# Starting TensorE on ones and loading x first in a two-layer attention kernel

## The chip, the cores and the metric

The kernel runs on 1 core of a Trainium2 chip. The metric is the device time of one execution in microseconds; three executions were timed, and one more was taken with the hardware profiler.

## The reference

Two attention layers follow one another on x (2 images of 32 x 32 positions and 256 channels, float32). One layer is:

```python
xn = group_norm(x, gamma, beta)                  # 32 groups of 8 channels
q, k, v = (xn @ w + b for w, b in ((wq, bq), (wk, bk), (wv, bv)))
attn = softmax(q @ k.T / sqrt(256))              # over the 1024 positions of an image
out = (attn @ v) @ wp + bp + x
```

## The kernel before

**Algebra.** Per layer A is made from wq and wk (with bk as one column more), Wx from wv and wp. The scores are xn times t, where t = A times xn plus a vector. V is xn times Wx. Each float32 operand of these products is split into a high and a low fp32r part: ScalarE writes the high part from PSUM, VectorE subtracts it for the low one. A product is then three fp32r matmuls. The products of weights themselves and the transposes are plain float32.

**Work.** A unit is one image in one layer (UNITS = 4), and has two chunks of 512 queries. Per unit: transpose the rows of x (four pieces r of 256 rows), statistics, group mean and variance by small matmuls into bank Z, gain and shift (affine_map), normalise in four quarters q = (h, k), xn_high and xn_low, four t products (h, k), eight values, and per chunk eight scores, the maxima, the exponentials and attention.

**Order.** Each engine has its own in-order list, written out by hand, and waits on semaphores. There are no loops that a planner orders. What matters here is the start, up to scores(0, 0) and the first transposes of image 1:

- SP (L238 to L245) loads wq and wk of layer 0, image 0 in four pieces, wv and wp, layer 1's wq and wk, wide(0) (bq, bk and bp of layer 0 on all partitions), layer 1's wv and wp, wide(1), image 1. Each is one DMA of 256 KB, wide 384 KB.
- TensorE (L806 to L837, then L969) transposes wq, the small vectors, wk, then the four pieces of x through ring[2] and ring[3] in turn, with A_product(0, 0) behind the third and A_product(0, 1) behind the fourth; then wv, wq(1) and wk(1), mean_of_groups, Wx_product(0, 0), variance_of_groups, Wx_product(0, 1), wv(1), output_bias of both layers, the A and the Wx products of layer 1, the four t products of unit 0, and scores(0, kb), with next_rows(1, kb) (transposes of image 1 into Z) behind each of the first four.
- ScalarE (L344 to L362, then L390) follows with weight_transposed (PSUM to SBUF), raw_rows, A_high, Wx_high, xn_high and t_high.
- VectorE (L557 to L585, then L637) follows with statistics_of, A_low, attention_vector, group_deviation, variance, affine_map, normalise(0) for all four quarters, Wx_low, the four xn_low, output_bias of both layers, attention_vector(1), A_low(1), Wx_low(1), and the four t_low of unit 0.
- GpSimd makes the constants, the power (L273) and, from the first output bias on, the eight residuals (L279) of unit 0.

t_product (L856) waits for the low parts of its half and takes four PSUM banks ring[0] to ring[3]. scores(0, kb) (L884) waits for t_low of its half. next_rows (L898) waits at r == 0 for both output biases on VectorE (L902), since these read Z.

Of the kernel before, what the change touches and what calls it, by code (L numbers as in the profile page):

```python
# [11 lines left out]
P = 128  # L12
# [7 lines left out]
def two_attention_layers(nc, x, layers, vectors, out):  # L20
# [13 lines left out]
    LAYERS = len(layers)  # L34
    UNITS = IMAGES * LAYERS
    KC = C // P
    NB = N // P
    HALVES = N // BANK
# [39 lines left out]
    with ExitStack() as ctx:  # L78
# [6 lines left out]
        def sem(name):  # L85
            return ctx.enter_context(nc.semaphore(name))
# [102 lines left out]
        ac_P = sem("ac_P")  # L189

        dv_const = sem("dv_const")
        dv_vec = sem("dv_vec")
# [28 lines left out]
        @block.sync  # L221
        def _(sp):
            def load_image(b):
                for r in range(NR):
                    sp.dma_start(xnat[:, b, 2 * r:2 * r + 2, :], x_rows[b, :, 2 * r:2 * r + 2, :]
                                 ).then_inc(ld_x[b][r], 16)

            def load_weights(l, names):
                for name in names:
                    sp.dma_start(w_raw[l, name][:], layers[l][name].rearrange("(k p) d -> p k d", p=P)  # L230
                                 ).then_inc(ld_w[l, name], 16)

            def load_wide(l):
                at = VECTORS.index(WIDE[0])
                sp.dma_start(wide[:, l], vectors_of_layer[:, l, at:at + len(WIDE), :].to_broadcast([P, len(WIDE), C])
                             ).then_inc(ld_wide[l], 16)

            load_weights(0, ("wq", "wk"))  # L238
            load_image(0)
            load_weights(0, ("wv", "wp"))  # L240
            load_weights(1, ("wq", "wk"))
            load_wide(0)
            load_weights(1, ("wv", "wp"))
            load_wide(1)
            load_image(1)  # L245

            for u in range(UNITS - IMAGES, UNITS):
                for i in range(NB):
                    sp.wait_ge(dv_O, u * NB + i + 1)
                    sp.dma_start(out_rows[u % IMAGES, :, i, :], xnat[:, u % IMAGES, i, :]).then_inc(stored, 16)  # L250
            sp.wait_ge(stored, 16 * IMAGES * NB)
# [57 lines left out]
        def _(act):  # L309
# [33 lines left out]

            weight_transposed(0, 0)  # L344
            weight_transposed(0, 1)
            for r in range(NR):
                raw_rows(0, r, ring[2 + r % 2])
                if r == 2:
                    A_high(0, 0)
            A_high(0, 1)  # L350
            weight_transposed(0, 2)
            weight_transposed(1, 0)
            weight_transposed(1, 1)
            for k in range(KC):
                Wx_high(0, k)
            weight_transposed(1, 2)
            for q in range(TQ):
                xn_high(0, q)
            A_high(1, 0)
            A_high(1, 1)  # L360
            for k in range(KC):
                Wx_high(1, k)  # L362

# [25 lines left out]

            for h in range(HALVES):  # L390
                for k in range(KC):
                    t_high(0, h, k)
            for kb in range(NB):
# [63 lines left out]
        @block.vector  # L457
        def _(dve):
            nc.vector.memset(minus_half[:], -0.5)
            for v in V:  # L460
# [80 lines left out]

            def normalise(v):
                dve.wait_ge(dv_stat, v * STAT + SHIFT)
                for q in range(TQ):
                    h, k = divmod(q, KC)
# [4 lines left out]
            def xn_low(v, q):  # L550
# [8 lines left out]
                                  ).then_inc(dv_vec, 1)  # L559
            statistics_of(0, 0)  # L560
            statistics_of(0, 1)
            statistics_of(0, 2)
            A_low(0, 0)
            statistics_of(0, 3)
            channel_statistics(0)
            A_low(0, 1)
            attention_vector(0, 0)
            group_deviation(0)
            attention_vector(0, 1)
            variance(0)  # L570
            Wx_low(0, 0)
            attention_vector(0, 2)
            affine_map(0)
            normalise(0)
            Wx_low(0, 1)
            for q in range(TQ):
                xn_low(0, q)
            for l in range(LAYERS):
                output_bias(l)
            for n in range(NATT):  # L580
                attention_vector(1, n)
            for k in range(KC):
                A_low(1, k)
            for k in range(KC):
                Wx_low(1, k)  # L585

# [49 lines left out]

            for h in range(HALVES):  # L637
                for k in range(KC):
                    t_low(0, h, k)
            for kb in range(1, NB):  # L640
# [107 lines left out]
        def _(pe):  # L748
# [22 lines left out]
            def Wx_product(l, mc):  # L771
                pe.wait_ge(ac_wT, 3 * l + 3)
                pe.wait_ge(ld_w[l, "wp"], 16)
                if l == 0:
                    pe.wait_ge(ac_xT, NR - KC + mc + 1)
                bank = ring[2 + mc][:, 0:C] if l == 0 else X[:, mc * C:(mc + 1) * C]
# [25 lines left out]
            def variance_of_groups(v):  # L802
                pe.wait_ge(dv_stat, v * STAT + VARC)
                nc.tensor.matmul(Z[:, 0:KC], group_mean[:], var_c[:], start=True, stop=True).then_inc(pe_gv, 1)

            pe.wait_ge(po_const, 5)  # L806
            transpose_weight(0, 0)
            pe.wait_ge(ld_vec, 16)
            for k in range(KC):
                last = nc.tensor.transpose(X[:, k * LAYERS * NV:(k + 1) * LAYERS * NV],  # L810
                                           vec_rows[:, k * P:(k + 1) * P], ident[0:LAYERS * NV, 0:LAYERS * NV])
            last.then_inc(pe_vec, 1)
            transpose_weight(0, 1)
            for r in range(NR):
                pe.wait_ge(ld_x[0][r], 16)
                if r >= 2:
                    pe.wait_ge(ac_xT, r - 1)
                transpose_rows(ring[2 + r % 2], 0, r)
                if r == 2:
                    A_product(0, 0)  # L820
            A_product(0, 1)
            transpose_weight(0, 2)
            transpose_weight(1, 0)
            transpose_weight(1, 1)
            mean_of_groups(0)
            Wx_product(0, 0)
            variance_of_groups(0)
            Wx_product(0, 1)
            transpose_weight(1, 2)
            pe.wait_ge(dv_stat, VARE)  # L830
            for l in range(LAYERS):
                output_bias(l)
            for mc in range(KC):
                A_product(1, mc)
            pe.wait_ge(ac_wT, 6)
            for mc in range(KC):
                Wx_product(1, mc)  # L837

# [17 lines left out]
            def t_product(u, h, k):  # L856
                l = u // IMAGES
                if k == 0:
                    pe.wait_ge(dv_xl, u * TQ + (h + 1) * KC)
                wait_for_bank("t", u, h, k)  # L860
                bank = bank_of("t", u, h, k)
# [106 lines left out]

            for h in range(HALVES):  # L969
                for k in range(KC):  # L970
                    t_product(0, h, k)
            for kb in range(NB):
# [96 lines left out]
```

## Time and profile before

| | us |
|---|---|
| median of 3 executions | 280.77 |
| lowest, highest | 280.07, 282.04 |
| profiled execution | 281.29 |
| its span, first to last instruction | 279.4 |
| mean granted TensorE clock | 0.988 |

The profiled execution's own time is 1.89 us longer than its span. Its durations and start times are those of that one execution. Start times below are microseconds from the span's start. PE is TensorE's matmul side, PEld its weight loads, DVE is VectorE, ACT is ScalarE, POOL is GpSimd, SP the engine that issues the loads. PEclk is the granted clock as a share of 2.4 GHz.

### The profile page before, as it was taken

The numbers are of one execution on the slowest core, as the hardware profiler recorded it, in microseconds if no ns is written. First come the engines' busy times: TensorE is split into PE (matmuls) and PEld (weight loads), VectorE is DVE, ScalarE is ACT, GpSimd is POOL, SyncE is SP. The second block draws the span as 40 slices with busy tenths as digits, with TensorE's granted clock in tenths as the row PEclk, the third lists the DMA queues.
The fourth block names the chain that finished last, engine by engine and source line by source line (L and its number), as shares of the span: only waits on it lengthen the run. The fifth ranks groups of instructions, "written<-read, shape, count | busy, mean of one in ns | idle before, by whom it ended". The sixth has DMA issues, their size and how long they took to land.

```text
span 279.4 us, 4591 instructions
## 1 busy us (share of the span) xinstructions
PE 261.8 (94%) x1650; PEld 235.6 (84%) x1650; DVE 176.3 (63%) x440; ACT 148.4 (53%) x291; POOL 110.6 (40%) x111
## 2 busy tenths in 40 slices
PE   3999999969987999999999999999999999999994
PEld 2887889849977899977998899977998899889993
DVE  0699568895568455755879455755978446564623
ACT  3564444757158734573377724573377615670660
POOL 2017101355135551552055651552055652560680
PEclk9999999996999999999999999999999999999999
DMA  5950000000000000000000000000000000100102
GB/s 163 366 188 1 0 1 2 0 0 2 0 0 4 1 0 2 0 0 2 1 0 1 2 2 0 0 2 0 33 27 19 1 21 19 38 2 19 40 19 75
DMA packets 5965, 7.37 MB, mean 26 GB/s; under 512 B 556, under 2 KB 4664, under 8 KB 5944
## 3 DMA queue, kind: packets, MB, share of 16 engines
q1 hardware_dynamic: 5920, 7.08, 7.5%
q8 instruction: 13, 0.21, 0.3%
q14 instruction: 8, 0.07, 0.1%
q10 hardware_dynamic: 24, 0.01, 0.0%
HBM read 4.99 MB, written 2.10 MB: 25 GB/s over the span
## 4 chain that ended last, share of the span: by engine, by line
PE 66%; DVE 21%; issue 6%; ACT 5%; DMA 1%; POOL 0%; DVEq 0%; ACTq 0%; POOLq 0%
PE ring L892 8%; PE ring L894 8%; PE ring L893 8%; PE O L931 7%; PE O L933 7%; PE O L932 7%; DVE xraw L547 4%; DVE S L625 3%; DVE xnat L635 3%; DVE xn_lo L554 2%; PE ring L878 2%; PE ring L931 2%; PE ring L933 2%; PE ring L932 2%; DVE t_lo L590 2%
## 5 line engine op out<-in xcount | busy, mean ns | idle before, releaser
L284 POOL TENSOR_TENSOR P_lo<-S,P_hi 128x512 fp32r<-128x512 f32 x64 | 83.0, 1303 | 118.3 <-ACT S L388 118.3
L931 PE MATMUL O<-V,P_hi 128*128 128x258 f32 x208 | 60.5, 291 | 0.0
L933 PE MATMUL O<-V,P_lo 128*128 128x258 f32 x208 | 59.4, 285 | 0.0
L932 PE MATMUL O<-V,P_hi 128*128 128x256 f32 x208 | 59.3, 285 | 0.0
L380 ACT COPY S<-ring 128x512 f32<-128x512 f32 x64 | 37.5, 586 | 39.7 <-PE ring L894 37.9
L387 ACT ACTIVATE P_hi<-S 128x512 fp32r<-128x512 f32 x64 | 40.5, 633 | 26.3 <-DVE S L625 26.3
L892 PE MATMUL ring<-t_hi,xn_lo 128*128 128x512 f32 x128 | 51.5, 403 | 0.8 <-DVE t_lo L590 0.8
L894 PE MATMUL ring<-t_hi,xn_hi 128*128 128x512 f32 x128 | 50.1, 392 | 0.0
L893 PE MATMUL ring<-t_lo,xn_hi 128*128 128x512 f32 x128 | 50.0, 391 | 0.0
L608 DVE TENSOR_TENSOR R<-ring,R 128x512 f32<-128x512 f32 x48 | 33.0, 687 | 25.4 <-ACT S L380 25.1
L625 DVE TENSOR_TENSOR S<-X,S 128x512 f32<-128x512 f32 x64 | 42.1, 681 | 0.0
L932 PEld LDWEIGHTS O<-V,P_hi 128*128 128x128 f32 x208 | 40.0, 192 | 0.5
L931 PEld LDWEIGHTS O<-V,P_hi 128*128 128x128 f32 x208 | 40.0, 192 | 0.5
L933 PEld LDWEIGHTS O<-V,P_lo 128*128 128x128 f32 x208 | 40.1, 193 | 0.0
L388 ACT ACTIVATE S<-S 128x512 f32<-128x512 f32 x64 | 39.8, 623 | 0.0
L892 PEld LDWEIGHTS ring<-t_hi,xn_lo 128*128 128x128 f32 x128 | 24.1, 188 | 5.5 <-DVE t_lo L590 1.2
L894 PEld LDWEIGHTS ring<-t_hi,xn_hi 128*128 128x128 f32 x128 | 24.0, 188 | 5.3
L893 PEld LDWEIGHTS ring<-t_lo,xn_hi 128*128 128x128 f32 x128 | 24.1, 189 | 4.3
L366 ACT ACTIVATE t_hi<-ring,att 128x512 fp32r<-128x512 f32 x16 | 10.7, 683 | 29.4 <-PE ring L867 29.4
L279 POOL TENSOR_TENSOR xnat<-xnat,out_bias 128x256 f32<-128x256 f32 x32 | 23.0, 751 | 6.3 <-DVE out_bias L500 6.3
L878 PE MATMUL ring<-Wx_hi,xn_lo 128*128 128x258 f32 x64 | 18.8, 294 | 2.8 <-DVE w_row L599 2.0
L590 DVE SCALAR_TENSOR_TENSOR t_lo<-ring,att,t_hi 128x512 fp32r<-128x512 f32 x16 | 11.7, 746 | 13.1 <-ACT t_hi L366 13.1
(113 smaller groups left out, 417.5 us busy)
## 6 DMA issues: line engine op xcount, KB each, us to landing
xnat<-in_x SPq DMA_DIRECT2D x8, 256.0 KB, 6.7
out<-xnat SPq DMA_DIRECT2D x16, 128.0 KB, 1.9
wide<-in_vectors SPq DMA_DIRECT2D x2, 384.0 KB, 6.9
w_wq<-in_L_conv_wq SPq DMA_DIRECT2D x2, 256.0 KB, 4.8
w_wk<-in_L_conv_wk SPq DMA_DIRECT2D x2, 256.0 KB, 4.8
w_wv<-in_L_conv_wv SPq DMA_DIRECT2D x2, 256.0 KB, 6.6
w_wp<-in_L_conv_wp SPq DMA_DIRECT2D x1, 256.0 KB, 6.7
w_wp<-in_L_conv_wo SPq DMA_DIRECT2D x1, 256.0 KB, 6.7
```

The lines of the kernel that those rows point to most:

```text
L284: nc.gpsimd.tensor_tensor(P_lo[:, tile, :], S[:, tile, :], P_hi[:, tile, :].bitcast(F32), ALU.subtract).then_inc(po_P, 1)
L380: nc.scalar.copy(S[:, tile_of(c, kb), :], bank_of("S", c, kb)[:]).then_inc(ac_S, 1)
L387: nc.scalar.activation(P_hi[:, tile, :], S[:, tile, :], ACT.Exp)
L388: nc.scalar.activation(S[:, tile, :], S[:, tile, :], ACT.Exp).then_inc(ac_P, 1)
L608: nc.vector.tensor_tensor(R[:], bank_of("S", c, kb)[:], earlier, ALU.max).then_inc(dv_R, 1)
L625: nc.vector.tensor_tensor(tile, X[:], tile, ALU.add).then_inc(dv_D, 1)
L892: nc.tensor.matmul(bank[:], xn_lo[:, kc, keys], t_hi[:, kc, cols], start=(kc == 0), stop=False)
L893: nc.tensor.matmul(bank[:], xn_hi[:, kc, keys], t_lo[:, kc, cols], start=False, stop=False)
L894: last = nc.tensor.matmul(bank[:], xn_hi[:, kc, keys], t_hi[:, kc, cols], start=False, stop=(kc == KC - 1))
L931: nc.tensor.matmul(bank[:, 0:C + 2], P_hi[:, tile, mine], v[:, kb, 0:C + 2], start=(kb == 0), stop=False)
L932: nc.tensor.matmul(bank[:, 0:C], P_hi[:, tile, mine], v[:, kb, C + 2:VX], start=False, stop=False)
L933: last = nc.tensor.matmul(bank[:, 0:C + 2], P_lo[:, tile, mine], v[:, kb, 0:C + 2], start=False, stop=(kb == NB - 1))
```

## The change

SP's order becomes image 0, wq and wk, wide(0), wv and wp, all of layer 1, wide(1), image 1. VectorE first of all writes ones into R[:, 0:P]; TensorE multiplies them with themselves (8 matmuls before anything else, 2 behind each of the first three pieces of x), with the result in Z, which nothing reads before it is written again. The pieces of x come first on TensorE and go to the four banks ring[0] to ring[3], then the three weights of layer 0 are transposed. In the order of TensorE, both A products stand around variance_of_groups; transposing wv(1) and both output_bias stand behind the first two t products, and Wx_product(1) behind the last two. The t products of unit 0 wait in addition for A_low (first half) and for Wx_low (second half). ScalarE and VectorE follow that order; normalise takes a list of quarters and is done in two parts. On VectorE both A_low stand ahead of affine_map, and output_bias and attention_vector(1) behind Wx_low(1). On ScalarE weight_transposed(1, 2) stands ahead of xn_high(0, 2).

```diff
@@ -188,6 +188,7 @@
         ac_S = sem("ac_S")
         ac_P = sem("ac_P")
 
+        dv_ones = sem("dv_ones")
         dv_const = sem("dv_const")
         dv_vec = sem("dv_vec")
         dv_A = sem("dv_A")
@@ -235,12 +236,11 @@
                 sp.dma_start(wide[:, l], vectors_of_layer[:, l, at:at + len(WIDE), :].to_broadcast([P, len(WIDE), C])
                              ).then_inc(ld_wide[l], 16)
 
+            load_image(0)
             load_weights(0, ("wq", "wk"))
-            load_image(0)
+            load_wide(0)
             load_weights(0, ("wv", "wp"))
-            load_weights(1, ("wq", "wk"))
-            load_wide(0)
-            load_weights(1, ("wv", "wp"))
+            load_weights(1, ("wq", "wk", "wv", "wp"))
             load_wide(1)
             load_image(1)
 
@@ -341,25 +341,21 @@
                 cols = slice(h * BANK, (h + 1) * BANK)
                 nc.scalar.copy(xn_hi[:, k, cols], xraw[:, k, cols]).then_inc(ac_xh, 1)
 
-            weight_transposed(0, 0)
-            weight_transposed(0, 1)
             for r in range(NR):
-                raw_rows(0, r, ring[2 + r % 2])
-                if r == 2:
-                    A_high(0, 0)
-            A_high(0, 1)
-            weight_transposed(0, 2)
+                raw_rows(0, r, ring[r])
+            for n in range(3):
+                weight_transposed(0, n)
+            for k in range(KC):
+                A_high(0, k)
             weight_transposed(1, 0)
             weight_transposed(1, 1)
+            xn_high(0, 0)
+            xn_high(0, 1)
             for k in range(KC):
                 Wx_high(0, k)
             weight_transposed(1, 2)
-            for q in range(TQ):
-                xn_high(0, q)
-            A_high(1, 0)
-            A_high(1, 1)
-            for k in range(KC):
-                Wx_high(1, k)
+            xn_high(0, 2)
+            xn_high(0, 3)
 
             def t_high(u, h, k):
                 act.wait_ge(pe_t, u * TQ + h * KC + k + 1)
@@ -387,9 +383,14 @@
                 nc.scalar.activation(P_hi[:, tile, :], S[:, tile, :], ACT.Exp)
                 nc.scalar.activation(S[:, tile, :], S[:, tile, :], ACT.Exp).then_inc(ac_P, 1)
 
-            for h in range(HALVES):
-                for k in range(KC):
-                    t_high(0, h, k)
+            for k in range(KC):
+                t_high(0, 0, k)
+            for k in range(KC):
+                A_high(1, k)
+            for k in range(KC):
+                t_high(0, 1, k)
+            for k in range(KC):
+                Wx_high(1, k)
             for kb in range(NB):
                 score_copy(0, kb)
                 if kb < NR:
@@ -456,6 +457,7 @@
 
         @block.vector
         def _(dve):
+            nc.vector.memset(R[:, 0:P], 1.0).then_inc(dv_ones, 1)
             nc.vector.memset(minus_half[:], -0.5)
             for v in V:
                 nc.vector.memset(v[:, :, C:C + 2].bitcast(F32), 1.0)
@@ -539,9 +541,9 @@
                 dve.wait_ge(dv_stat, at + GMUL)
                 nc.vector.tensor_tensor(shift[:], beta, gain_mean[:], ALU.subtract).then_inc(dv_stat, 1)
 
-            def normalise(v):
+            def normalise(v, quarters=range(TQ)):
                 dve.wait_ge(dv_stat, v * STAT + SHIFT)
-                for q in range(TQ):
+                for q in quarters:
                     h, k = divmod(q, KC)
                     cols = slice(h * BANK, (h + 1) * BANK)
                     nc.vector.tensor_scalar(xraw[:, k, cols], xraw[:, k, cols], gain[:, k:k + 1], shift[:, k:k + 1],
@@ -557,32 +559,25 @@
             dve.wait_ge(pe_vec, 1)
             nc.vector.tensor_copy(vec_cols[:], X[:, 0:KC * LAYERS * NV].rearrange("p (k r) -> p k r", k=KC)
                                   ).then_inc(dv_vec, 1)
-            statistics_of(0, 0)
-            statistics_of(0, 1)
-            statistics_of(0, 2)
+            for r in range(NR):
+                statistics_of(0, r)
+            channel_statistics(0)
+            group_deviation(0)
+            attention_vector(0, 0)
+            variance(0)
             A_low(0, 0)
-            statistics_of(0, 3)
-            channel_statistics(0)
             A_low(0, 1)
-            attention_vector(0, 0)
-            group_deviation(0)
+            affine_map(0)
+            normalise(0, range(0, 2))
+            xn_low(0, 0)
+            xn_low(0, 1)
             attention_vector(0, 1)
-            variance(0)
-            Wx_low(0, 0)
+            normalise(0, range(2, 4))
+            for k in range(KC):
+                Wx_low(0, k)
+            xn_low(0, 2)
+            xn_low(0, 3)
             attention_vector(0, 2)
-            affine_map(0)
-            normalise(0)
-            Wx_low(0, 1)
-            for q in range(TQ):
-                xn_low(0, q)
-            for l in range(LAYERS):
-                output_bias(l)
-            for n in range(NATT):
-                attention_vector(1, n)
-            for k in range(KC):
-                A_low(1, k)
-            for k in range(KC):
-                Wx_low(1, k)
 
             def t_low(u, h, k):
                 dve.wait_ge(ac_t, u * TQ + h * KC + k + 1)
@@ -634,9 +629,18 @@
                 rows = xnat[:, (c // 2) % IMAGES, (c % 2) * QB + j, :]
                 nc.vector.scalar_tensor_tensor(rows, bank[:, 0:C], inv, rows, ALU.mult, ALU.add).then_inc(dv_O, 1)
 
-            for h in range(HALVES):
-                for k in range(KC):
-                    t_low(0, h, k)
+            for k in range(KC):
+                t_low(0, 0, k)
+            for k in range(KC):
+                A_low(1, k)
+            for k in range(KC):
+                t_low(0, 1, k)
+            for k in range(KC):
+                Wx_low(1, k)
+            for l in range(LAYERS):
+                output_bias(l)
+            for n in range(NATT):
+                attention_vector(1, n)
             for kb in range(1, NB):
                 running_max(0, kb)
                 if kb <= NR:
@@ -771,8 +775,6 @@
             def Wx_product(l, mc):
                 pe.wait_ge(ac_wT, 3 * l + 3)
                 pe.wait_ge(ld_w[l, "wp"], 16)
-                if l == 0:
-                    pe.wait_ge(ac_xT, NR - KC + mc + 1)
                 bank = ring[2 + mc][:, 0:C] if l == 0 else X[:, mc * C:(mc + 1) * C]
                 for kd in range(KC):
                     last = nc.tensor.matmul(bank, wvT[:, l, kd, mc * P:(mc + 1) * P],
@@ -803,38 +805,38 @@
                 pe.wait_ge(dv_stat, v * STAT + VARC)
                 nc.tensor.matmul(Z[:, 0:KC], group_mean[:], var_c[:], start=True, stop=True).then_inc(pe_gv, 1)
 
+            def keep_running(n):
+
+                for _ in range(n):
+                    nc.tensor.matmul(Z[:, 0:P], R[:, 0:P], R[:, 0:P], start=True, stop=True)
+
+            pe.wait_ge(dv_ones, 1)
+            keep_running(8)
             pe.wait_ge(po_const, 5)
-            transpose_weight(0, 0)
-            pe.wait_ge(ld_vec, 16)
-            for k in range(KC):
-                last = nc.tensor.transpose(X[:, k * LAYERS * NV:(k + 1) * LAYERS * NV],
-                                           vec_rows[:, k * P:(k + 1) * P], ident[0:LAYERS * NV, 0:LAYERS * NV])
-            last.then_inc(pe_vec, 1)
-            transpose_weight(0, 1)
             for r in range(NR):
                 pe.wait_ge(ld_x[0][r], 16)
-                if r >= 2:
-                    pe.wait_ge(ac_xT, r - 1)
-                transpose_rows(ring[2 + r % 2], 0, r)
-                if r == 2:
-                    A_product(0, 0)
+                transpose_rows(ring[r], 0, r)
+                if r == 0:
+                    pe.wait_ge(ld_vec, 16)
+                    for k in range(KC):
+                        last = nc.tensor.transpose(X[:, k * LAYERS * NV:(k + 1) * LAYERS * NV],
+                                                   vec_rows[:, k * P:(k + 1) * P], ident[0:LAYERS * NV, 0:LAYERS * NV])
+                    last.then_inc(pe_vec, 1)
+                if r < NR - 1:
+                    keep_running(2)
+            transpose_weight(0, 0)
+            transpose_weight(0, 1)
+            transpose_weight(0, 2)
+            mean_of_groups(0)
+            A_product(0, 0)
+            variance_of_groups(0)
             A_product(0, 1)
-            transpose_weight(0, 2)
             transpose_weight(1, 0)
             transpose_weight(1, 1)
-            mean_of_groups(0)
-            Wx_product(0, 0)
-            variance_of_groups(0)
-            Wx_product(0, 1)
-            transpose_weight(1, 2)
-            pe.wait_ge(dv_stat, VARE)
-            for l in range(LAYERS):
-                output_bias(l)
+            for mc in range(KC):
+                Wx_product(0, mc)
             for mc in range(KC):
                 A_product(1, mc)
-            pe.wait_ge(ac_wT, 6)
-            for mc in range(KC):
-                Wx_product(1, mc)
 
             def wait_for_bank(*tile):
 
@@ -857,6 +859,12 @@
                 l = u // IMAGES
                 if k == 0:
                     pe.wait_ge(dv_xl, u * TQ + (h + 1) * KC)
+                if u == 0:
+
+                    if h == 0:
+                        pe.wait_ge(dv_A, KC)
+                    else:
+                        pe.wait_ge(dv_Wx, KC)
                 wait_for_bank("t", u, h, k)
                 bank = bank_of("t", u, h, k)
                 cols = slice(h * BANK, (h + 1) * BANK)
@@ -966,9 +974,16 @@
                         wait_for_output_bank(c, j)
                     attend(c, j, kb)
 
-            for h in range(HALVES):
-                for k in range(KC):
-                    t_product(0, h, k)
+            for k in range(KC):
+                t_product(0, 0, k)
+            transpose_weight(1, 2)
+            pe.wait_ge(dv_stat, VARE)
+            for l in range(LAYERS):
+                output_bias(l)
+            for k in range(KC):
+                t_product(0, 1, k)
+            for mc in range(KC):
+                Wx_product(1, mc)
             for kb in range(NB):
                 scores(0, kb)
                 if kb < NR:
```

## Rows read from the trace of the kernel before

**Rows 1.** The page: busy share of the span by engine, and TensorE in 40 slices.

```profile
PE 261.8 (94%) x1650; PEld 235.6 (84%) x1650; DVE 176.3 (63%) x440; ACT 148.4 (53%) x291; POOL 110.6 (40%) x111
...
PE   3999999969987999999999999999999999999994
```

**Rows 2.** Busy time by stretch, TensorE: stretch, length, PE busy, PEclk, DMA share, GB/s.

```profile
7.30:10.20 2.90, 2.88 (x13) 1.00 1.02 352
59.30:61.80 2.50, 0.06 (x1) 0.94 0.00 0
61.80:68.40 6.60, 6.47 (x29) 0.50 0.01 2
```

**Rows 3.** Groups of weight loads (count, busy us, mean ns), then transposes in time order.

```profile
L758 PEld LDWEIGHTS O<-ident,w_wq 128*128 128x128 f32 x4 | 0.7, 216 | 3.7 <-issue 3.7
...
L793 PEld LDWEIGHTS ring<-ident,xnat 128*128 128x128 f32 x12 | 2.3, 221 | 1.8 <-DMA xnat<-in_x 1.5 <-issue 0.3
...
L793 PEld LDWEIGHTS ring<-ident,xnat 128*128 128x128 f32 x4 | 0.5, 140 | 0.1
...
11.07 0.60 PE L793 MATMUL ring<-ident,xnat 128*128 128x128 f32 x4
...
12.38 0.60 PE L758 MATMUL X<-ident,w_wv 128*128 128x128 f32 x4
...
12.82 0.60 PE L758 MATMUL O<-ident,w_wq 128*128 128x128 f32 x4
```

**Rows 4.** DMA: first piece of the chain, landing of x, volume from 0.

```profile
0.79 2.84 DMA w_wq<-in_L_conv_wq
...
DMA to landing us min/median/max: 5.5/6.7/7.6
...
0.00:6.60 6.60, 2.45 (x10) 1.71 (x10) 0.47 (x10) 2.22 (x3) 1.91 (x11) 1.00 0.57 155
0.00:10.10 10.10, 5.23 (x23) 4.21 (x24) 1.39 (x13) 3.63 (x5) 1.91 (x11) 1.00 0.71 220
```

**Rows 5.** Instructions in time order on TensorE: start, duration, form, idle time before.

```profile
18.12 1.90 PE L767 MATMUL O<-wkT_bk,wqT 128*128 128x257 f32 x8
19.86 1.89 PE L778 MATMUL X<-w_wp,wvT 128*128 128x256 f32 x8
21.39 0.58 PE L865 MATMUL ring<-xn_hi,A_lo 128*128 128x512 f32 x1
...
28.11 0.50 PE L892 MATMUL ring<-t_hi,xn_lo 128*128 128x512 f32 x1 [0.79 <-DVE t_lo L590]
```

**Rows 6.** The same on ScalarE and VectorE, from the third piece of x.

```profile
11.27 0.38 ACT L327 ACTIVATE A_hi<-ring 128x256 fp32r<-128x256 f32 x1 [0.36 <-PE ring L767]
11.75 0.42 DVE L478 SCALAR_TENSOR_TENSOR A_lo<-ring,A_hi 128x256 fp32r<-128x256 f32 x1
13.11 0.39 DVE L506 BATCH_NORM_AGGREGATE mv<-bn 128x2 f32<-128x24 f32 x2
14.54 0.16 DVE L518 TENSOR_TENSOR var_c<-dev,mv 128x2 f32<-128x2 f32 x1
...
16.24 0.16 DVE L529 TENSOR_TENSOR r0sq<-r 128x2 f32<-128x2 f32 x1
16.59 0.59 ACT L322 COPY wvT<-X 128x512 f32<-128x512 f32 x1
17.41 1.92 DVE L547 TENSOR_SCALAR xraw<-xraw,gain,shift 128x512 f32<-128x512 f32 x4
18.00 1.14 ACT L342 CAST xn_hi<-xraw 128x512 fp32r<-128x512 f32 x2 [0.82 <-DVE xraw L547]
```

**Rows 7.** The same, behind Wx(1).

```profile
21.78 0.65 ACT L334 CAST Wx_hi<-X 128x256 fp32r<-128x256 f32 x2 [0.94 <-PE X L778]
21.98 0.75 DVE L500 TENSOR_TENSOR out_bias<-Z,wide 128x256 f32<-128x256 f32 x2
...
26.00 0.74 DVE L487 TENSOR_TENSOR Wx_lo<-X,Wx_hi 128x256 fp32r<-128x256 f32 x2
```

## The prediction

> **What bounds the kernel now.** I read the page first: its busy line and its slices. TensorE (PE) is busy 94% of 279.4 us, and the slices show 9 tenths nearly everywhere; only the first and the last are low, and a few others a little [rows 1]. The change touches only what lies before the scores of the first unit, so the second view is the busy time by stretch. PE is idle until 3.8 and for 1.1 us before 7.3, works without a gap from there to 27.3, lacks 0.8 us before 28.11 [rows 5], and is then full until 59.3. A second hole of 2.4 us stands before 61.8, and behind it the granted clock is 0.50, the 1.2 GHz level, until 68.4 [rows 2]. So from 7.3 on the bound of the start is PE's own queue, and the end can come earlier only if scores(0, 0) starts before 28.11 us, or if less stands behind it.
>
> Third, the groups of weight loads by line, since they pace transposes. A load of a transpose takes 216 to 221 ns until 9.9 us and 140 ns from 10.8 us on; four of them stand 0.44 us after one another's start at the fast pace (12.38 and 12.82) [rows 3]. The granted clock is printed as 1.00 in both [rows 2], but the longer loads tell me the lower level, 1.2 GHz, before some 10.2 us. So four transposes take 0.9 us of PE at the lower level and 0.44 at the higher.
>
> **The change part by part.** The sum is made against the profiled execution: 281.29 us with a span of 279.4. The median of the runs shown is 280.77, so 0.52 is taken off at the end.
>
> *DMA order.* x now stands at the head of SP's queue, wq and wk behind it, then wide(0), wv and wp, then layer 1. An issue costs 0.43 to 0.5 us, as before, and the same bytes move. Lower bound for x0: the first transfer in the queue landed 2.84 us after its issue at 0.79, so 3.63 us [rows 4]. Upper bound: the transfers of x took 5.5 us at best, so 6.3 us. By volume: before, 6.6 us x 155 GB/s = 1.02 MB had moved by 6.6 us, which is all of x (1.05 MB) [rows 4]. I take the volume; x then keeps ahead of PE (below). wv of layer 0 ends at 2.23 MB, and 10.1 us x 220 GB/s is 2.22: it is there at 10.1 [rows 4].
>
> *Ones.* keep_running(8) is 8 fp32 matmuls of 128 columns. Two A products, four such calls, show as eight instructions [rows 5], so these are 16, each paced like a transpose: 16 x 0.227 = 3.6 us at the lower level, from about 1.05 (DVE writes the ones first of all) to 4.7. Three keep_running(2) add 4 instructions each, 0.44 us at the higher level, 0.91 at the lower. When does the clock rise? Two cases in the trace: PE dense from 7.3, fast by 10.2, 2.9 us; PE dense from 61.8, fast by 68.4, 6.6 us [rows 2]. From 1.05 that gives 4.0 to 7.7; I take the middle, 5.8. Until the last group of x, PE has 3 groups of x, 3 of ones (6 x 0.44) and the vectors (0.2): 2.9 us at the higher level. From 4.7, with 1.1 us at half speed, that puts the last transposes of x at 8.15 (7.3 for a rise at 4.0; 9.05 for 7.7; 10.5 if it doesn't rise in time). Before they were at 11.07 [rows 3]. So the head gains 2.9 us. x3 has landed by volume at 6.7: the ones cover the landing, and if it is late instead (6.3 for x0), the last group is at about 9.3.
>
> *From x to the first t product.* From those transposes to the aggregated statistics: 11.07 to 13.50 (13.11 + 0.39), 2.43 us, unchanged [rows 3, 6]. wq, wk and wv are transposed meanwhile (1.3 us) and are in. Statistics to var_c: 13.50 to 14.70 (14.54 + 0.16), 1.2 us [rows 6]. Then comes something new: VectorE takes both A_low ahead of affine_map. A_product(0, 1) stands behind variance_of_groups, so A(0, 1) ends 2.35 after the statistics (two products of 4 x 0.217 = 0.87, as eight take 19.86 - 18.12 = 1.74, with two small matmuls and the tail); A_high 0.38 + 0.17 and A_low 0.42 + 0.15 less overlap bring affine_map to 3.4, where before it was 16.24 - 13.50 = 2.7 [rows 5, 6]. The power on GpSimd ends earlier and isn't seen. Affine_map takes 1.17 us (16.24 to 17.41), xn_high starts 0.59 behind it (18.00), two of them take 1.14, the second xn_low 0.6: 2.35 [rows 6]. Now only two quarters are normalised ahead. In all 2.43 + 3.4 + 1.17 + 2.35 and hops = 9.5 us; before 21.39 - 11.07 = 10.3. t(0,0) starts at 17.65, 3.7 us earlier. From A(0, 1) to there PE has two weights to transpose, the pair of Wx and the pair of A(1), 0.88 + 1.73 + 1.74 = 4.35 us, in the 4.9 that it has: no bound.
>
> *Behind the first t products.* Before, four t products (24 matmuls, 27.3 less 21.39, 5.6) and the hole of 1.2 led to 28.11, 6.7 us [rows 5]. Now: two t products 2.78, the transposes of wv(1) 0.44, output_bias 1.73 (8 instructions), two t products 2.78, Wx(1) 1.73 = 9.5 us. The work is only moved: 3.9 us that stood ahead of the t products now stand between them and the scores. And it adds a wait. ScalarE has weight_transposed(1, 2) ahead of xn_high(0, 2) in its strict order, and that copy now waits for transposes that stand behind both first t products. So xn_high(0, 2) can't begin until 0.16 + 0.59 after them, then two xn_high 1.14 and an xn_low 0.6 with hops: 2.6 us, against 1.73 of output_bias as cover [rows 5, 6]. PE waits 0.85 us at t(1,0). Queued behind that copy on ScalarE are also both t_high, on VectorE both t_low and all A_low(1); their covers (4.5 us of PE) suffice. In sum 10.3 us: scores(0, 0) at 27.95, 0.15 us earlier than before.
>
> *Behind the scores' start.* next_rows(1, 0) writes bank Z and waits for VectorE's two output biases, which now stand behind Wx_low(1), which needs the last Wx product: 0.16 tail, Wx_high 0.65, Wx_low 0.7, output_bias 0.7, hops: 2.25 us after scores(0, 0) starts. The scores take 1.39, so PE waits 0.85; before, they were done by 22.7 [rows 7]. The three attention_vector(1) that follow on VectorE hold up the first running maximum by under 1 us; a bank waits for it only at the sixth scores, some 5 us later: nothing. GpSimd's eight residuals, also behind the first output bias, start near 30 rather than 22.5 and are done long before its next work: nothing.
>
> **Sum.** -0.15 + 0.85 = +0.7 us. 281.29 + 0.7 = 282.0 in the profiled execution's terms; less 0.52, 281.5. From 41 us on all is as before, shifted.
>
> *A page against this.* The rows: PE did nothing but transposes of x from 7.3 to about 10, and then ran at the higher level [rows 2, 3]. The Trainium skill's page "TensorE: Matmul & The Clock Gate", Part 4 (PE-mode transpose), says that transposes don't count as activity as matmuls do, and that the fast clock doesn't engage for them. By that rule only the ones would raise the clock. By the rows transposes suffice; the trace disagrees with the page.
>
> **Rivals.**
> - *The clock stays low through the transposes of x* (slower side). The ones end at 4.7, and if what follows, half transposes, doesn't bring the rise before the products of A, the last transposes of x stand at 10.5, 2.35 later than I take; some of it is PE work that would follow anyway. 282.0 + 2.35 = 284.4, less 0.52: 283.8. For it: the first stretch of PE work, from 3.8 to 6.3, transposes too, didn't raise it. Against: the second did, alone. It decides once the rise comes after 8 us. A late x (x3 after 8 us) ends at the same place: +1.2 to +2.
> - *The head gains in full*: the clock rises at 4.0, x0 lands at 3.63, x3 transposed at 7.3; -0.85 on the sum: 280.6. Some executions of before may have a later rise than the profiled one, which adds up to a microsecond in favour of the change: 279.6.
> - *The hole at 59.3 to 61.8 no longer drops the clock*, since it comes at another moment. The stretch at 0.50 from 61.8 to 68.4 costs 3.3 us of PE, half of 6.6 [rows 2]. That would be 281.5 - 3.3 = 278.2. For it: nothing but that a fall followed a single hole of 2.4 us. Against: the hole comes from VectorE's normalise of image 1, which keeps its place.
> - *The two new waits are hidden*, because copies run faster than their rows: 281.5 - 1.7 = 279.8. Against: both are chains of strict queues and their rows hardly vary.
>
> **How the numbers follow.** My forecast 0.50; clock low or x late 0.17; full gain of the head 0.17; waits hidden 0.08; clock kept at the hole 0.08. A measurement of this kernel tells about 1% (2.8 us) from no change. Faster by over 1% (under 278.0) needs the hole's clock and some more: 0.08. Slower by over 1% (over 283.6) is half and more of the first rival: 0.11. Same 0.81. The range: down to 278.8, which leaves the hole out, up to 283.8, the end of the slower rival. The forecast's own range is 280.6 (rise at 4.0) to 282.4 (rise at 7.7).
>
> **What would show it.** Right: weight loads of the ones at 227 ns falling to about 140 by 6 us; the last transposes of x near 8.2; t(0,0) near 17.7; PE idle 0.85 us at the third t product with ScalarE's xn_hi late, and 0.85 us ahead of the first transposes into Z, released by out_bias; scores(0, 0) near 28. Wrong: ones that end after 5 us at the slow pace and transposes of x past 10 us (the first rival), PE waiting for xnat's transfers, no idle time at the third t product, or a granted clock of 1.00 through 61 to 68 us.

## The result and the profile after

The changed kernel took 285.18 us (median of 4, 282.94 to 286.7) against 281.24 before: ratio 1.0145, 95% interval 1.0102 to 1.0188. Four more executions, run beside the experiments, gave 1.0132 (1.0106 to 1.0157). It is about 1.4% slower. Forecast were 281.5 us and a range to 283.8, so the time was wrong, and so was the likeliest outcome, no change by the prediction's own line of 1%. Ratios leave out executions over 1.5% above the fastest of the same kernel (one of two_waits_mended and two of all_mended_no_ones below); medians are of all. The profiled execution took 284.60 us with a span of 282.7, 3.3 us more than before.

The page of the changed kernel has a fuller first slice of PE than before (8 tenths, 3 before [rows 1]), a second one that is less full (6, 9 before), and one slice of PEclk more that isn't full. Slices 1 and 2 hold the start, 7.1 us each.

```profile
PE   8698899996988999999999999999999999999994
...
PEclk9899999997999999999999999999999999999999
```

TensorE's instructions of the changed kernel in time order, up to the first scores (start, duration, form, idle time before and who ended it):

```profile
1.10 3.78 PE L811 MATMUL Z<-R 128*128 128x128 f32 x16 [1.10 <-DVE R L460]
...
8.01 0.64 PE L795 MATMUL ring<-ident,xnat 128*128 128x128 f32 x4
8.85 0.66 PE L762 MATMUL O<-ident,w_wq 128*128 128x128 f32 x4 [0.20 <-DMA w_wq<-in_L_conv_wq]
9.72 0.65 PE L762 MATMUL O<-ident,w_wk 128*128 128x128 f32 x4 [0.21 <-DMA w_wk<-in_L_conv_wk]
12.13 1.11 PE L762 MATMUL X<-ident,w_wv 128*128 128x128 f32 x4 [1.76 <-DMA w_wv<-in_L_conv_wv]
13.04 0.43 PE L802 MATMUL Z<-mv,group_mean 128*128 128x2 f32 x2
...
21.24 0.50 PE L873 MATMUL ring<-xn_hi,A_lo 128*128 128x512 f32 x1 [0.33 <-DVE xn_lo L556]
...
27.25 0.50 PE L873 MATMUL ring<-xn_hi,A_lo 128*128 128x512 f32 x1 [0.79 <-DVE xn_lo L556]
...
31.68 0.58 PE L900 MATMUL ring<-t_hi,xn_lo 128*128 128x512 f32 x1
...
34.27 0.63 PE L795 MATMUL Z<-ident,xnat 128*128 128x128 f32 x4 [0.85 <-issue]
```

The ones come first, and the last four transposes of x stand at 8.01 (11.07 before, [rows 3]). Until here the change gives its 3 us. Then TensorE stands still for 1.76 us until wv lands, and mean_of_groups is behind it at 13.04. The scores start at 31.68, where before they did at 28.11 [rows 5]. The chain of waits has the same: it runs through the transfer of wv, which no step of the chain before did at this place, and not through the statistics:

```profile
4.16 7.92 DMA w_wv<-in_L_conv_wv
12.09 0.04 issue
12.13 1.11 PE X L762 x4
13.25 0.22 PE Z L802 x2
13.46 1.92 PE ring L771 x4
...
15.60 0.99 PE ring L771 x4
16.61 0.39 ACT A_hi L327
...
17.09 0.42 DVE A_lo L480
```

Behind the mean it goes on through the two A products, which are queued behind wv too, and through A_high and A_low, which the change put ahead of affine_map; the first product takes 1.92 us at the lower clock, the second 0.99, by then at the higher. So what the late wv holds is this whole queue, not the mean alone.

The statistics were ready at 10.49, 2.5 us before the first mean matmul. VectorE's rows of the changed kernel show what it waited for:

```profile
10.10 0.39 DVE L508 BATCH_NORM_AGGREGATE mv<-bn 128x2 f32<-128x24 f32 x2
13.50 0.16 DVE L514 COPY gmean<-Z 128x2 f32<-128x2 f32 x1 [3.02 <-PE Z L802]
```

And the pause has a price beyond its length. Busy time of TensorE by stretch (length, PE busy, granted clock, DMA share, GB/s), changed kernel; the first stretch is the pause, the last two lie at the hole that stood at 59.3 to 61.8 before [rows 2]:

```profile
10.40:12.10 1.70, 0.00 (x0) 0.98 1.07 371
12.10:15.50 3.40, 3.37 (x13) 0.51 1.07 385
15.50:21.20 5.70, 5.42 (x29) 1.00 0.34 130
...
64.60:66.70 2.10, 0.15 (x1) 0.99 0.00 0
66.70:70.10 3.40, 3.18 (x14) 0.50 0.00 0
```

For 3.4 us behind the pause the clock is at its lower level, 1.2 GHz, and does there what takes 1.7 us at the higher one. At the later hole it is low for 3.4 us rather than 6.6. So the account of the two profiled executions closes: the first transposes of image 1 came at 34.27 where before they did at 29.61, 4.7 us later; the hole gave back (6.6 - 3.4) / 2 = 1.6; 3.1 are left, and the time is 3.3 us longer. What the hole gave back is a matter of the execution, not of the change: most executions of the kernel before that ran beside the experiments have a mean granted clock of 0.992 or 0.993, its profiled one 0.988.

### The profile page after: what moved, and what is told of

The parts are those of the page before. It is cut to its first block, busy times and chain, and to the rows that moved or that the text cites. A ratio compares the mean times of both kernels' runs of the same rounds, so it can differ in the third digit from the quotient of the medians.

```text
span 282.7 us, 4648 instructions
## 1 busy us (share of the span) xinstructions
PE 265.4 (94%) x1678; PEld 238.6 (84%) x1678; DVE 177.9 (63%) x441; ACT 148.2 (52%) x291; POOL 110.7 (39%) x111
## 4 chain that ended last, share of the span: by engine, by line
PE 69%; DVE 18%; ACT 6%; DMA 3%; issue 3%; SPq 1%; DVEq 0%; ACTq 0%
PE ring L900 8%; PE ring L902 8%; PE ring L901 8%; PE O L939 7%; PE O L941 7%; PE O L940 7%; DVE xraw L549 3%; DVE S L620 3%; DMA w_wv<-in_L_conv_wv 3%; DVE xnat L630 3%; DVE xn_lo L556 3%; PE ring L873 2%; PE ring L886 2%; PE ring L875 2%; PE ring L939 2%
## 5 line engine op out<-in xcount | busy, mean ns | idle before, releaser
L362 ACT ACTIVATE t_hi<-ring,att 128x512 fp32r<-128x512 f32 x16 | 10.6, 683 | 26.9 <-PE ring L875 26.9
```

## The experiments

All are edits of the changed kernel but the last two: before_with_ones edits the kernel before, changed_again is unedited. Ratios are to the kernel before, run on the same chip (281.2 to 281.3 us). The first four ran on one chip, the next four on a second, the last two on a third, so that ratios compare better than medians between these groups. The theory (W in the expectations): wv lands late, the statistics stand behind its transposes, and the pause lowers the clock.

**mean_ahead_of_wv.** The copy on ScalarE moves with the transposes.

```diff
-            transpose_weight(0, 2)
             mean_of_groups(0)
             A_product(0, 0)
             variance_of_groups(0)
             A_product(0, 1)
+            transpose_weight(0, 2)
```

> The changed kernel (285.2 us, ratio 1.0145 to the kernel before), with the transposes of wv(0) and their copy moved behind both A products, so that mean_of_groups(0) waits for nothing from DMA. Theory W (the late landing of wv holds the statistics, and the pause lowers the clock): no idle time at 10.4 to 12.1, clock stays at 1.00, scores(0, 0) about 3 us earlier (28.5 rather than 31.7), time 281.5 to 282.5, ratio about 1.003. Rival M (what the change moved behind the t products costs it, whatever stands ahead): less than 1 us gained, ratio about 1.012.

Measured: 281.72 us, 1.0023 (0.9999 to 1.0047). In its trace the mean comes at 10.91, wv's transposes at 13.17 without idle time, and the scores at 28.61; the clock of the stretches is 1.00:

```profile
10.91 0.35 PE L803 MATMUL Z<-mv,group_mean 128*128 128x2 f32 x2 [0.68 <-DVE mv L509]
...
13.17 0.60 PE L763 MATMUL X<-ident,w_wv 128*128 128x128 f32 x4
...
24.17 0.50 PE L874 MATMUL ring<-xn_hi,A_lo 128*128 128x512 f32 x1 [0.79 <-DVE xn_lo L557]
...
28.61 0.58 PE L901 MATMUL ring<-t_hi,xn_lo 128*128 128x512 f32 x1
```

```profile
12.10:15.50 3.40, 3.34 (x23) 1.00 1.04 377
```

As W had it: the scores start within 0.2 us of its 28.5. One position in the order carries 3.5 us, the whole loss within the measurement. The edit takes wv's transposes from ahead of the mean and of both A products at once, so it doesn't tell their shares apart.

**ones_in_the_gap.** The pause stays and is filled with ones.

```diff
+            keep_running(1)
             transpose_weight(0, 0)
+            keep_running(1)
             transpose_weight(0, 1)
+            keep_running(8)
             transpose_weight(0, 2)
```

> The changed kernel with ten more multiplications of ones: one ahead of wq(0), one ahead of wk(0), eight ahead of wv(0), where TensorE waits for transfers. They fill the pause and shorten no wait. Theory W, if half of its price is the clock: wv is still transposed at 12.1, but the clock doesn't fall, and scores(0, 0) start 1.5 us earlier than 31.7; time 283.5, ratio 1.008. Rival (the wait alone costs, the clock nothing): unchanged, 285. Rival (idle time doesn't set the clock): it falls nonetheless, unchanged.

Measured: 284.07 us, 1.0108 (1.0076 to 1.0141). Its profiled execution has no fall at 12 us. The ones hold wv's transposes up a little, to 12.41 (12.13 in the changed kernel); the scores start at 30.31, 1.4 us earlier than there:

```profile
12.10:15.50 3.40, 3.40 (x26) 1.00 1.05 364
```

```profile
10.62 1.95 PE L811 MATMUL Z<-R 128*128 128x128 f32 x16
12.41 0.60 PE L762 MATMUL X<-ident,w_wv 128*128 128x128 f32 x4
...
30.31 0.58 PE L903 MATMUL ring<-t_hi,xn_lo 128*128 128x512 f32 x1
```

So the loss has, most likely, two parts: about 1.1 to 1.4 us of clock, and 2.3 us of wait that these ones didn't shorten (284.07 against 281.72). The second is what the times show. The first is less sure. The timed difference to the changed kernel, 1.1 us, lies within overlapping intervals, and one trace without a fall is no proof, since two_waits_mended below has one with the pause unfilled. For it speak the mean granted clocks: 4 of these 6 executions have 0.992 or more, against 1 of the 8 of the changed kernel.

**wide_behind_wv.** The transfer of wide(0) moves behind wv and wp.

```diff
-            load_wide(0)
             load_weights(0, ("wv", "wp"))
+            load_wide(0)
```

> The changed kernel with wide(0) loaded behind wv(0) and wp(0) instead of ahead of them. Theory W, with landing set by the bytes queued ahead: wv lands about 1 us earlier (384 KB at 370 GB/s), at 11.1; mean_of_groups 1 us earlier, perhaps no fall of the clock; ratio 1.005 to 1.010. But attention_vector(0, 0) on VectorE waits for wide ahead of variance and may take the gain back. Rival (wv is late for another reason than wide): wv still at 12.

Measured: 281.59 us, 1.0022 (0.9998 to 1.0047), more than the expected gain. In the profiled execution wv lands 6.24 us after its issue at 3.63, so at 9.87, 2.2 us earlier and not 1, for 384 KB less in front of it:

```profile
9.24 0.66 PE L762 MATMUL O<-ident,w_wk 128*128 128x128 f32 x4
9.92 0.66 PE L762 MATMUL X<-ident,w_wv 128*128 128x128 f32 x4
10.47 0.35 PE L802 MATMUL Z<-mv,group_mean 128*128 128x2 f32 x2
```

The wait for wide on VectorE that I feared did come, 0.76 us long, but it held up nothing that shows: behind it the second A_low still waited 0.20 us for ScalarE.

```profile
12.24 0.42 DVE L495 CUSTOM_DVE_ANT_0 products<-w_wk,wide 128x256 f32<-128x256 f32 x1 [0.76 <-DMA wide<-in_vectors]
...
13.40 0.42 DVE L480 SCALAR_TENSOR_TENSOR A_lo<-ring,A_hi 128x256 fp32r<-128x256 f32 x1 [0.20 <-ACT Wx_hi L328]
```

This is the second, independent removal of the pause, from the DMA side, with the same result as the first. How early wv lands varies, though: in the profiled execution of best, with the same order of transfers, it lands at 10.90.

**no_ones.** All ones and the memset are taken out.

> The changed kernel without any multiplication of ones. Theory W: the ones buy a fast clock from 5.2 us, which only makes TensorE wait longer for wv; without them x is transposed at the landing of its pieces, all by about 9, and wv still lands at 12.1: scores(0, 0) within 0.5 us of 31.7 and the time unchanged, 285, ratio 1.012 to 1.016. Rival (the ones carry a gain that the rest of the change gives back): 1 to 2 us slower, ratio 1.02.

Measured: 284.61 us, 1.0123 (1.0095 to 1.0152), as the changed kernel. Its transposes wait for x's pieces, and the last stand at 8.04, against 8.01 with the ones; wv is late all the same, and the scores start at 31.63:

```profile
5.90 1.97 PE L794 MATMUL ring<-ident,xnat 128*128 128x128 f32 x8 [0.17 <-DMA xnat<-in_x]
8.04 1.11 PE L794 MATMUL ring<-ident,xnat 128*128 128x128 f32 x4 [0.18 <-DMA xnat<-in_x]
...
12.03 1.12 PE L761 MATMUL X<-ident,w_wv 128*128 128x128 f32 x4 [0.66 <-DMA w_wv<-in_L_conv_wv]
```

The ones bought nothing here. The head's 3 us are those of the new DMA order, not of the fast clock. The clock stayed at its lower level here until after 15 us, by the pace of its instructions (four transposes take 1.12 us at 8.98 and 0.60 at 16.36, an A product 2.06 at 13.22 and 1.16 at 15.36), and in the changed kernel it was back at that level from 12.1 to 15.5: what the ones had given, the pause took away.

```profile
8.98 1.12 PE L761 MATMUL O<-ident,w_wq 128*128 128x128 f32 x4
...
13.22 2.06 PE L770 MATMUL ring<-wkT_bk,wqT 128*128 128x257 f32 x4
...
15.36 1.16 PE L770 MATMUL ring<-wkT_bk,wqT 128*128 128x257 f32 x4
16.36 0.60 PE L761 MATMUL O<-ident,w_wq 128*128 128x128 f32 x4
```

The printed granted clock doesn't show this: it reads 1.00 for these stretches, as it did at the start of the kernel before.

**two_waits_mended.** The two waits that the prediction priced at 0.85 us each are removed, wv is left as it is. On ScalarE the copy of wv(1) goes behind xn_high, on VectorE the output biases go ahead of A_low(1):

```diff
-            weight_transposed(1, 2)
             xn_high(0, 2)
             xn_high(0, 3)
+            weight_transposed(1, 2)
...
             for k in range(KC):
                 t_low(0, 0, k)
+            for l in range(LAYERS):
+                output_bias(l)
```

> The changed kernel (1.0145) with two places mended and the wait for wv left in: ScalarE copies wv(1) behind xn_high(0, 3) instead of ahead of xn_high(0, 2), and VectorE adds both output biases right behind the first two t_low. Theory T (the two predicted waits are real cost, 0.8 us each, added to what wv costs): no idle time ahead of the third t product or of the first transposes into Z, 1.6 us less, about 283.5, ratio 1.009. Rival (behind the late wv they are hidden or come back at the next wait): under 0.5 us, ratio 1.013.

Measured: 281.38 us, 1.0001 (0.997 to 1.0033); 3.8 us less than the changed kernel's 285.18, where 1.6 were expected. Both idle times are gone: the transposes into Z start 1.58 us after the scores, 2.59 in the changed kernel. But TensorE waits 2.13 us for wv, and in the profiled execution the clock didn't fall there:

```profile
12.08 0.66 PE L762 MATMUL X<-ident,w_wv 128*128 128x128 f32 x4 [2.13 <-DMA w_wv<-in_L_conv_wv]
...
28.99 0.58 PE L900 MATMUL ring<-t_hi,xn_lo 128*128 128x512 f32 x1
...
30.57 0.60 PE L795 MATMUL Z<-ident,xnat 128*128 128x128 f32 x4
```

Of its 12 executions 5 have a mean granted clock of 0.982 to 0.987 and a median of 282.35; 4 have 0.992 to 0.994 and 281.1; 3 have 0.998 or 0.999 and 279.8. All four of changed_again lie at 0.982 to 0.988. So a good part of the surplus is that the clock fell less often. Nothing in the edit stands ahead of the pause, so I can't say why. The changed kernel has 8 executions in all and none on this chip, so chance or the chip may have a part; that stays open. Nor does the length of a pause decide alone: the later hole, 2.45 us long here and in wide_behind_wv, passed without a fall in the profiled executions of both, where 2.44 us brought one in the kernel before. What the two waits cost is shown by the next experiment.

**all_mended.** mean_ahead_of_wv and these two edits together.

> mean_ahead_of_wv (1.0023) with the same two places mended. If the three costs add up: 1.6 us less than 281.7, about 280.1, ratio 0.996 to 0.998, scores(0, 0) at 27.8. Rival (the order of the change has a bound of its own, TensorE's total work): nothing more than 1.000.

Measured: 280.0 us, 0.9968 (0.9943 to 0.9994). Against mean_ahead_of_wv that is 1.7 us by the medians and 1.5 by the ratios for the two waits, as expected (1.6); the scores start at 27.30 in its profiled execution.

**all_mended_no_ones.** all_mended without the ones and their memset.

> all_mended without any ones. Theory W says that the ones were worth nothing in the changed kernel because the wait for wv swallowed what they gave. With the wait gone they should be worth their fast clock: without them x is done at 8.5 to 9 and all up to the first A products runs at the lower level, 1.5 to 3 us later: ratio 1.003 to 1.006 where all_mended has 0.997. Rival (the ones are worth nothing anywhere, x's landing sets the pace): equal to all_mended within 0.002.

Measured: 280.5 us, 0.9981 (0.9949 to 1.0013). The ones are worth 0.5 us by the medians, which the intervals don't separate from nothing. The profiled execution starts the scores at 30.66, 3.4 us behind all_mended's, which is more than its median shows: one execution of each is no measure of this. In it the last piece of x was late as well, its transposes starting at 8.89 and not at 8.26, and the clock was at its lower level until after 16 us. The expected 1.003 to 1.006 lies outside the interval, so that expectation missed; the rival (equal within 0.002) fits.

```profile
8.89 1.12 PE L795 MATMUL ring<-ident,xnat 128*128 128x128 f32 x4 [0.73 <-DMA xnat<-in_x]
```

**best.** all_mended with wide(0) behind wv and wp.

> all_mended with wide(0) loaded behind wv and wp of layer 0. wide_behind_wv gained 3.6 us on its own by letting wv land before 9.9; with mean_of_groups ahead of wv that is no longer needed, so equal to all_mended or up to 0.5 us less by the later Wx products: ratio 0.995 to 0.997. If wide_behind_wv gained mainly by keeping the clock up at the hole near 62 us, this shows it too: the granted clock stays at 1.00 there and the ratio falls under 0.993.

Measured: 279.6 us, 0.9947 (0.9922 to 0.9971), the fastest version run and 0.5% ahead of the kernel before. Its order of transfers adds nothing that its interval separates from all_mended. The mean granted clock is 0.988 to 0.994 in 10 of 12 executions, and the profiled one has it at 0.50 from 63.1 to 66.5 us, so this order of transfers doesn't keep the clock up at the later hole.

**before_with_ones.** The kernel before, with dv_ones, the memset and this at TensorE's head:

```diff
+            pe.wait_ge(dv_ones, 1)
+            for _ in range(8):
+                nc.tensor.matmul(Z[:, 0:P], R[:, 0:P], R[:, 0:P], start=True, stop=True)
             pe.wait_ge(po_const, 5)
```

> The kernel before with nothing but the eight multiplications of ones ahead of the first transposes. They end at 4.7 and put wq's transposes 0.9 us later, which nothing waits for, and TensorE still idles from about 6.5 to 7.3 for x. If the ones' worth is a fast clock for the first transposes of x and the first A product, the clock is up at 5 instead of 10.3 and everything from x0 on comes up to 1.4 us earlier: ratio 0.995 to 0.997. If x's landing sets the pace there too, below 0.5 us: 0.998 to 1.000. If the idle time ahead of x lowers the clock again, 1.000.

Measured: 280.54 us, 0.9972 (0.9948 to 0.9996). In the profiled execution the clock was up from 4.7 us on and stayed up although TensorE waited 1.45 us for x; the scores start at 27.72, 0.4 us earlier than before. The ones alone give 0.3%.

```profile
7.57 0.66 PE L795 MATMUL ring<-ident,xnat 128*128 128x128 f32 x4 [1.45 <-DMA xnat<-in_x]
...
27.72 0.50 PE L897 MATMUL ring<-t_hi,xn_lo 128*128 128x512 f32 x1 [0.78 <-DVE t_lo L592]
```

**changed_again.** The changed kernel, unedited.

> The changed kernel once more, unedited, for the clock and time of more executions beside before's. If it is the pause for wv that lowers the clock, the executions fall into groups by mean granted clock, about 1.7 us apart for each half per cent; the ones near 0.98 have the fall at 12 us and the one at 62 us. Ratio 1.012 to 1.018.

Measured: 285.28 us, 1.0132 (1.0106 to 1.0157), granted clock 0.982 to 0.988. In its profiled execution wv's transposes wait 1.23 us until 12.77, and the clock falls there too (0.50 from 13 to 14 us). Four executions are too few to see groups. The lowest of the first four, 282.94 us, is the one with a clock of 0.993.

## Why the prediction was wrong

**The head, right.** The ones ended at 4.7 as worked out, the clock rose between the first and the second piece of x, from 4.7 to 6.2 (5.8 taken), and the last transposes of x stood at 8.01 (8.15 taken). That the ones are what makes it so was wrong: no_ones has the same time.

**The step that failed: "wv of layer 0 ends at 2.23 MB, and 10.1 us x 220 GB/s is 2.22: it is there at 10.1".** It landed at 12.09. The volume itself was right to the digit. By 10 us the changed kernel had moved 10 x 219 GB/s = 2.19 MB:

```profile
0.00:10.00 10.00, 8.49 (x53) 7.81 (x54) 3.43 (x19) 4.08 (x6) 1.91 (x11) 1.00 0.73 219
```

What failed is the reading of a volume as a landing. The transfers of this queue overlapped: when wv was complete, at 12.09, the changed kernel had moved 2.96 MB, 0.73 MB more than what ends with wv. The trace of before had it. x0 ended at 0.79 MB of the queue and TensorE waited for it until 7.3, though 1.02 MB had moved by 6.6 us [rows 4] and 0.79 MB by some 5.6. I had the row that says so, x's landings of 5.5 to 7.6 us after issue [rows 4], and used it for x alone, where it was harmless. wv took 7.92 us from its issue at 4.16.

How long the lag is could not have been read off so surely. It was 1.7 us for x0 before, but before's own wv (it ends at 1.84 MB, moved by 9.1 us) landed at 10.26, 1.1 us behind. With 1.1 wv would be due here at 11.2, with 1.7 at 11.8. It measured 1.9, and in the seven other profiled executions with this order of transfers 1.3 (all_mended) to 2.2 (changed_again). With wide behind wv it was 1.0 (wide_behind_wv) and 2.1 (best). What sets it stays open. Even with the shortest of these wv would have landed at 11.1, and TensorE was through with wk's transposes at 10.4.

**What it set off.** The prediction said of wq, wk and wv only that they "are in"; mean_of_groups and both A products were queued behind wv's transposes on TensorE, and with them the whole chain to affine_map. It gave no price for the case that wv is late. The price: mean at 13.04 rather than about 10.6, 2.4 us, and the 1.2 GHz stretch from 12.1 to 15.5. t(0, 0) came at 21.24 instead of 17.65, 3.6 us. A rival had the clock staying low through the transposes of x; it was the clock falling again at a pause behind them. Another had the clock kept at the later hole: the changed kernel's trace has a fall there, of 3.4 us.

**The rest, right.** From the first t product to the scores 31.68 - 21.24 = 10.4 us (10.3). The two new waits are 0.79 and 0.85 us (0.85 each); all_mended shows that they are real cost, 1.7 us. With wv's wait taken out by mean_ahead_of_wv the kernel takes 281.72 us where the sum without such a wait gave 281.5. The sum was right but for one term, of 3.5 us. That it comes so near is partly luck: in mean_ahead_of_wv's profiled execution the first transposes of image 1 start at 31.20, 1.6 us later than before where the sum had 0.7, and a later hole with 3.4 us at the lower clock, not 6.6, gives 1.6 back.

```profile
31.20 0.63 PE L796 MATMUL Z<-ident,xnat 128*128 128x128 f32 x4 [0.85 <-issue]
```

Two readings were off without effect: the four t products last 5.9 us to the end of the last one (27.3 less 21.39) and the hole behind them is 0.79, where the prediction has 5.6 and 1.2, with the same sum; and TensorE has 4.7 us from A(0, 1) to the first t product, not 4.9.

**The rule on transposes.** The rule of the Trainium skill's page "TensorE: Matmul & The Clock Gate", Part 4 (PE-mode transpose), is that the fast clock doesn't engage for transposes. The runs are divided on it. Against it: in the kernel before the clock rose by 10.8 us, with only transposes and one A product, begun at 10.08, since 7.32. And in before_with_ones, where the ones had raised the clock, TensorE had only transposes to do from 7.57 to about 9.5, and they ran at the higher level (0.66 us for four). For it: in no_ones TensorE had only transposes to do from 4.33 to 12.9, with waits of at most 0.66 us, and the clock was at its lower level until after 15 us, when the A products were under way; in all_mended_no_ones it was the same until after 16. So the prediction's "by the rows transposes suffice" held for the one execution that it was read from, and what decides stays open.

## What to carry to other kernels

When a load order is changed, take each transfer's landing from the landings in the trace, not from the bytes moved: here wv's completion lagged the volume by 1.0 to 2.2 us, so leave room for it. Then ask of each wait on a transfer what is queued behind it on that engine; a matmul that needs no transfer belongs ahead of one that does. In ones_in_the_gap dummy work in the wait gave back 1.1 us of the 3.5, and the wait itself stayed; at the head of the changed kernel ones bought nothing, since the clock fell again at the next pause, and in before_with_ones they gave 0.3%. A single trace was a poor measure of the clock: the same hole of 2.4 us lowered it in some executions and not in others.

## What the runs showed of the hardware that I had not expected

- A pause of TensorE of 1.76 us, with short ones of 0.2 us before it, was followed by 3.4 us at 1.2 GHz; one of 2.13 us in two_waits_mended was not, and neither was the hole of 2.45 us near 62 us in wide_behind_wv. The same pause costs up to 1.7 us more in one execution than in the next.
- So times of one kernel go with its mean granted clock: all_mended took 278.1 to 278.4 us at 0.998 or 0.999 and 280.6 to 281.3 at 0.988.
- Moving one transfer of 384 KB from ahead of wv to behind it brought wv at least 2.2 us earlier, where its bytes at 370 GB/s are 1.1 us.
